# Expert rows weighted as they leave PSUM, routing weights scattered to the rows' places, and gathers that add into the residual

## The reference, cut to what matters

```python
logits = xt @ gate_w                       # xt = rmsnorm(h), 1024 tokens, 8 experts
topv, topi = jax.lax.top_k(logits, 2)
probs = jax.nn.softmax(topv, axis=-1)      # two weights for each token
for e in range(8):                         # F = 1024
    hh = jax.nn.silu(xt @ w1[e]) * (xt @ w3[e])
    out = out + w[:, e:e+1] * (hh @ w2[e])  # w holds the token's weight for e, or 0
x = layernorm(x + h + out)
```

## Time and profile before

| | us |
|---|---|
| median of 3 runs | 1451.32 |
| the runs | 1441.35, 1451.32, 1457.49 |
| profiled execution | 1436.41 |
| its span | 1434.8 |

### The profile page before, as it was taken

How to read it: one execution, slowest core, us unless ns; L and a number is a source line. 1 busy time by engine, 2 the same in 40 slices (tenths; PEclk the granted TensorE clock), 3 DMA queues, 4 the chain that set the end, 5 groups by cost and what they waited for, 6 DMA issues and landing times. The chain is left out here.

```text
span 1434.8 us, 24588 instructions
## 1 busy us (share of the span) xinstructions
PE 1318.0 (92%) x7943; PEld 716.3 (50%) x7943; DVE 1023.8 (71%) x1966; ACT 809.0 (56%) x1460; POOL 367.8 (26%) x602
## 2 busy tenths in 40 slices
PE   7988999999999999998687999999866999999993
PEld 4444444444444444443344555555434566666771
DVE  5847777777777777778568787888677655666676
ACT  5547666666666666666427566665653453455552
POOL 5402020201010111103256465664334100000025
PEclk9999999999999999999699999999987999999997
DMA  8317676657675767588264353535474765777653
GB/s 251 60 37 146 134 126 121 146 111 148 117 153 105 151 115 150 108 184 145 98 206 71 71 143 61 132 70 97 87 201 149 247 216 198 235 237 235 221 144 122
DMA packets 451869, 206.18 MB, mean 144 GB/s; under 512 B 401089, under 2 KB 415425, under 8 KB 451777
## 3 DMA queue, kind: packets, MB, share of 16 engines
q1 hardware_dynamic: 448640, 196.67, 57.7%
q0 software_dynamic: 2560, 8.39, 1.8%
q10 hardware_dynamic: 576, 0.00, 0.0%
HBM read 87.38 MB, written 16.45 MB: 72 GB/s over the span
## 5 line engine op out<-in xcount | busy, mean ns | idle before, releaser
L1453 DVE SCALAR_TENSOR_TENSOR X<-xa_SC,xa_rs,X 128x1024 f16<-128x1024 f32 x128 | 164.4, 1284 | 98.3 <-issue 97.6
L1276 ACT ACTIVATE X<-xa_SC,xa_rs 128x1024 f16<-128x1024 f32 x128 | 147.1, 1149 | 110.5 <-POOL xa_rs L1007 110.5
L1145 PE MATMUL xa_psS<-xa_KT,xa_QT 128*128 128x512 f16 x768 | 186.4, 379 | 6.1 <-DVE xa_mn L1485 4.7
L1157 PE MATMUL xa_psO<-wide,xa_V 128*128 128x512 f16 x768 | 173.6, 383 | 7.0 <-DMA wide<-X 6.9
L1007 POOL TENSOR_SCALAR xa_rs<-xa_rc,flag 128x1 f32<-128x1 f32 x128 | 33.9, 265 | 517.0 <-DVE xa_rc L1446 517.0
L1485 DVE CUSTOM_DVE_ANT_0 xa_SC<-xa_psS,maskb 128x1024 f32<-128x1024 f32 x128 | 155.1, 1212 | 4.5 <-PE xa_psS L1145 2.4
L1298 ACT ACTIVATE xa_SC<-xa_SC,xa_mn 128x1024 f32<-128x1024 f32 x128 | 145.5, 1136 | 13.4 <-DVE xa_mn L1485 13.3
L1157 PEld LDWEIGHTS xa_psO<-wide,xa_V 128*128 128x128 f16 x768 | 74.6, 98 | 102.2 <-issue 17.1
L1145 PEld LDWEIGHTS xa_psS<-xa_KT,xa_QT 128*128 128x128 f16 x768 | 73.4, 98 | 90.7 <-DVE xa_mn L1485 9.4
L1298 ACT ACTIVATE sa_SC<-sa_SC,sa_mn 128x128 f32<-128x128 f32 (+3 forms) x128 | 71.5, 558 | 78.1 <-DVE sa_mn L1485 78.0
L1944 PE MATMUL rmoe_psG<-rmoe_XGT,W 128*128 128x352 f16 (+6 forms) x768 | 109.0, 292 | 2.1 <-DVE rmoe_XGT L2052 2.1
(11 more groups left out here) (291 smaller groups left out, 2271.7 us busy)
## 6 DMA issues: line engine op xcount, KB each, us to landing
first<-in_L_ffn_w_dram SPq DMA_DIRECT2D x12, 2048.0 KB, 11.6
W2raw<-in_L_ffn_w_dram SPq DMA_DIRECT2D x8, 2048.0 KB, 9.1
expert_rows_dram<-zeros SPq DMA_DIRECT2D x10, 512.0 KB, 9.4
xa_WPraw<-in_L_xattn_Wq_dram SPq DMA_DIRECT2D x8, 512.0 KB, 11.1
xa_WOraw<-in_L_xattn_Wo_dram SPq DMA_DIRECT2D x8, 512.0 KB, 4.5
first<-in_L_ffn_wq_dram SPq DMA_DIRECT2D x4, 1024.0 KB, 7.6
first<-in_L_ffn_wo_dram SPq DMA_DIRECT2D x4, 1024.0 KB, 5.8
first<-in_L_ffn_w_dram SPq DMA_DIRECT2D x8, 512.0 KB, 6.8
```

Of the source, the lines that this page charges most:

```text
L1145: last = nc.tensor.matmul(psS[j % NSC][:, c:c + cw], QT[b][:, hq, g, t * P:(t + 1) * P], KT[b][:, hk, c:c + cw], start=(q == 0), stop=(q = ...
L1157: last = nc.tensor.matmul(psO[:, c:], V[b][:, hv, blk, :], PT[g % NPT][:, blk, hp, c:], start=(blk + q == 0), stop=(blk == NBLK - 1 and q ...
L1276: nc.scalar.activation(PN[j % NPN][:, 0:w // P, 0, :], by_block(SC[j % NSC], w), ACT.Identity, scale=rs[:, j % 4:j % 4 + 1]).then_inc(norm ...
L1453: nc.vector.scalar_tensor_tensor(out=PN[j % NPN][:, 0:w // P, 1, :], in0=by_block(SC[j % NSC], w), scalar=rs[:, j % 4:j % 4 + 1], in1=PN[j ...
```

## The change

The routing weight is multiplied into an expert's rows when they are copied out of PSUM, instead of when they are added to the residual.

- For this the weights have to stand in the order of the expert's rows. The first WT_ROWS = 5 rows of XG (2560 numbers) become a list of weights, and all rows of experts move up by 5. POOL issues 16 more scatters of one number for each of 128 tokens, ahead of the 16 scatters of rows.
- SP reads the list back into `row_wt`, one DMA for each of the 20 row tiles of experts 0 to 6 (`TILES_BEFORE[LAST]`), one number for each partition. They stand after the first loads of w1 and w3 and ahead of its wait for `scattered`.
- VectorE's copy of psY becomes a multiplication by `row_wt`; where `packs`, one more multiplication follows the addition. Before the first of them it waits for the 20 loads.
- The 16 gathers add into X directly (`compute_op=ALU.add`). All eight of choice 0 come first, then all of choice 1, each waiting for the earlier gather of its tile; in the first eight each waits for the one four tiles back.
- `combine` and its 16 instructions are gone; `finish_rows(t)` waits for the two gathers of tile t.
- One more clearing DMA of 5 rows of YG stands in the attention stage before.

```diff
-FIRST_ROW = tuple(sum(CAPS[:p]) for p in range(E))
+WT_ROWS = -(-sum(CAPS) // (D - 1))
+FIRST_ROW = tuple(WT_ROWS + sum(CAPS[:p]) for p in range(E))
...
+        row_wt = sb("row_wt", [P, LAST, CTL], F32)
+        WG = XG.rearrange("n d -> (n d)")[0:WT_ROWS * D].rearrange("(n o) -> n o", o=1)
...
+            def load_weights(p):
+
+                for r in range(TILES[p]):
+                    at, w = FIRST_ROW[p] + r * P, width(p, r)
+                    sp.dma_start(row_wt[0:w, p, r:r + 1], WG[at:at + w, :]).then_inc(wt_in, 16)
...
                     if first:
+                        sp.wait_ge(wt_scattered, 16 * 2 * NT)
+                        for q in range(LAST):
+                            load_weights(q)
                         sp.wait_ge(scattered, 16 * 2 * NT)
                         sp.wait_ge(pad_zeroed, 1)
                     load_rows(p + 1)
...
             pool.wait_ge(slots_done, 1)
             for t in range(NT):
                 for k in range(2):
+                    pool.indirect_dma_start(out=WG, out_offset=bass.IndirectOffsetOnAxis(ap=slots[:, k, t:t + 1], axis=0),
+                                            in_=p12[:, k, t:t + 1], in_offset=None).then_inc(wt_scattered, 16)
+            for t in range(NT):
+                for k in range(2):
                     pool.indirect_dma_start(out=XG, out_offset=bass.IndirectOffsetOnAxis(ap=slots[:, k, t:t + 1], axis=0),
                                             in_=XPF[:, t, :], in_offset=None).then_inc(scattered, 16)
...
-            for t in range(NT):
-                if t >= 2:
-                    pool.wait_ge(gathered[t - 2], 32)
-                for k, dst in enumerate((Y1, Y2)):
-                    pool.indirect_dma_start(out=dst[:, t, :], out_offset=None, in_=YG[0:ROWS, :],
...
+            for k in range(2):
+                for t in range(NT):
+                    if k:
+                        pool.wait_ge(gathered[t], 16)
+                    elif t >= 4:
+                        pool.wait_ge(gathered[t - 4], 16)
+                    pool.indirect_dma_start(out=X[:, t, :], out_offset=None, in_=YG[0:ROWS, :],
+                                            in_offset=bass.IndirectOffsetOnAxis(ap=slots[:, k, t:t + 1], axis=0),
+                                            compute_op=ALU.add).then_inc(gathered[t], 16)
...
-            def combine(t, ks=(0, 1)):
-
-                for k in (ks,) if isinstance(ks, int) else ks:
-                    dve.wait_ge(gathered[t], 32)
-                    wait_from(dve, combined, 2 * t + k)
-                    nc.vector.scalar_tensor_tensor(out=X[:, t, :], in0=(Y1, Y2)[k][:, t, :], scalar=p12[:, k, t:t + 1],
-                                                   in1=X[:, t, :], op0=ALU.mult, op1=ALU.add).then_inc(combined, 1)
...
                     if first and r == 0:
                         dve.wait_ge(x_added, NT)
+                        dve.wait_ge(wt_in, 16 * TILES_BEFORE[LAST])
...
-                        nc.vector.tensor_tensor(YR[0:w, r, :], psY[r % 2][0:w, :], folded[0:w, :],
-                                                ALU.add).then_inc(y_copied, 1)
+                        nc.vector.tensor_tensor(folded[0:w, :], psY[r % 2][0:w, :], folded[0:w, :],
+                                                ALU.add).then_inc(summed, 1)
+                        dve.wait_ge(summed, i + 1)
+                        nc.vector.tensor_scalar(YR[0:w, r, :], folded[0:w, :], wt, None, ALU.mult).then_inc(y_copied, 1)
                     else:
-                        nc.vector.tensor_copy(YR[0:w, r, :], psY[r % 2][0:w, :]).then_inc(y_copied, 1)
+                        nc.vector.tensor_scalar(YR[0:w, r, :], psY[r % 2][0:w, :], wt, None, ALU.mult).then_inc(y_copied, 1)
...
+        cleared.append((YG[0:WT_ROWS, :], zeros[0:WT_ROWS, :], zeroed))
```

More of the change, by code:

```diff
@@ L34 @@
 CAPS = (352, 352, 336, 304, 288, 272, 256, 240)
-FIRST_ROW = tuple(sum(CAPS[:p]) for p in range(E))
+WT_ROWS = -(-sum(CAPS) // (D - 1))
+FIRST_ROW = tuple(WT_ROWS + sum(CAPS[:p]) for p in range(E))
 TILES = tuple(-(-c // P) for c in CAPS)
 TILES_BEFORE = tuple(sum(TILES[:p]) for p in range(E + 1))
-ROWS = sum(CAPS)
+ROWS = WT_ROWS + sum(CAPS)
 PINNED = 16384.0
@@ L1910, in _ @@
             pool.wait_ge(scattered, 16 * 2 * NT)
-            for t in range(NT):
-                if t >= 2:
-                    pool.wait_ge(gathered[t - 2], 32)
-                for k, dst in enumerate((Y1, Y2)):
-                    pool.indirect_dma_start(out=dst[:, t, :], out_offset=None, in_=YG[0:ROWS, :],
-                                            in_offset=bass.IndirectOffsetOnAxis(ap=slots[:, k, t:t + 1], axis=0)
-                                            ).then_inc(gathered[t], 16)
+            for k in range(2):
[7 more added lines that the diff above has]
+                                            compute_op=ALU.add).then_inc(gathered[t], 16)
             for i in range(NT):
@@ L2096, in step @@
                                                 ALU.is_equal).then_inc(chosen_done, 1)
-                if last:
-                    for t in range(3):
-                        combine(t)
                 for r in range(TILES[p]):
@@ L2104, in step @@
                                                 YH[0:width(p, r), r, 0, :], ALU.subtract).then_inc(y_lo, 1)
-                        if r == 0:
-                            for t in range(3, 6):
-                                combine(t)
-                        else:
+                        if r:
                             finish_rows(r - 1)
@@ L2121, in step @@
                         dve.wait_ge(folded_done, i + 1)
-                        nc.vector.tensor_tensor(YR[0:w, r, :], psY[r % 2][0:w, :], folded[0:w, :],
-                                                ALU.add).then_inc(y_copied, 1)
+                        nc.vector.tensor_tensor(folded[0:w, :], psY[r % 2][0:w, :], folded[0:w, :],
+                                                ALU.add).then_inc(summed, 1)
+                        dve.wait_ge(summed, i + 1)
+                        nc.vector.tensor_scalar(YR[0:w, r, :], folded[0:w, :], wt, None, ALU.mult).then_inc(y_copied, 1)
                     else:
-                        nc.vector.tensor_copy(YR[0:w, r, :], psY[r % 2][0:w, :]).then_inc(y_copied, 1)
+                        nc.vector.tensor_scalar(YR[0:w, r, :], psY[r % 2][0:w, :], wt, None, ALU.mult).then_inc(y_copied, 1)
             def finish_rows(t):
                 dve.wait_ge(part_ready, t + 1)
-                dve.wait_ge(combined, 2 * t + 2)
+                dve.wait_ge(gathered[t], 32)
                 nc.vector.scalar_tensor_tensor(out=X[:, t, :], in0=part_bank[t][:, :], scalar=last_wt[:, t:t + 1],
@@ L2182, in _ @@
             for t in range(TILES[LAST] - 1, NT):
-                if t + 5 < NT:
-                    combine(t + 5)
                 finish_rows(t)
```

7 lines of the change are left out of this document (4 added, 3 removed).

## The result

| | before | changed |
|---|---|---|
| median, us | 1451.09 (20 runs, 1441.35 to 1457.49) | 1454.71 (20 runs, 1450.64 to 1463.16) |
| profiled execution, us | 1436.41 | 1457.36 |
| its span, us | 1434.8 | 1455.8 |

The changed kernel takes 1.0042 [1.0028, 1.0057] of the time before: 3.6 us more by the medians, within 1%. The forecast was 1455, 4 us more. The two profiled executions stand 21 us apart, though, and the rest of this document is about that gap. The forecast met the median, but what the traces show before expert 1 and in the tail is not what it priced.

What follows compares the result with a forecast made beforehand. TensorE was taken to bound nearly all, VectorE the tail after the last up stage. Tail -4.4, stall +6.8 and clock +1.7 sum to +4.1 us: 1451.3 + 4 = 1455 us, range 1446 to 1468.

Steps and rivals of the forecast that it cites:

- So the tail gives -4.4 us, if the gathers are in time: After the last up stage: without the 16 combines the eighth `finish_rows` starts at 1418.8 instead of 1423.23.
- from below it costs what a plain one costs: POOL in the tail: lower assumption for a gather that adds, taken at 1.25 us for each issue.
- gathers that add are the bound: Rival, chance 0.14: in the tail `finish_rows` waits for slow gather transfers; with the stall +14 to +26 us, 1465 to 1478.
- POOL's queue of scatters: POOL before expert 1: weights from 1092.48, row scatters moved past 16 issues, from 1117.0 to a last start at 1137.8.
- Now 20 weight loads come first: SP's queue before expert 1's row loads: 20 weight loads take 7.8 us, to 1136.4, hidden behind the scatters.
- Weights of four bytes are dear: Rival, chance 0.08: a weight load costs SP 1.0 us, +11 us, 1462; at 2.0, +31.
- The stall before expert 1: TensorE waits for `turned` before expert 1: 6.8 us, from a shift of 10.4 less 3.6 of room.
- 1.7 for the clock: TensorE's first matmuls of expert 1 after the wait run at the 1.2 GHz level: +1.7 us.
- The lower bound of 0.5 us for the stall: Low end of the 0.5 to 17.5 us range given for TensorE's stall before expert 1.
- Costs put at nothing: VectorE's multiplications, the W2raw load of expert 1 issued 3.5 us later against TensorE, and the clearing DMA: no cost.
- Checks it set itself: Wrong if idle before expert 1 is under 2 or over 12 us, or the tail's chain names the gathers.
- Three of its other signs: SP's row loads first issued at 1141 to 1142; tail 4.4 us shorter; no VectorE wait for an indirect DMA.

Runs made afterwards that it cites:

- e_no_weights: Changed kernel without the weight scatters and loads, `row_wt` filled with a constant (routing weights left out): 1437.63 us, 1.0013 of the kernel before.
- e_nw_early: As e_no_weights, with the adding gathers no longer waiting for the middle of the last up stage: 1434.40 us, 0.9901 of the kernel before.
- e_pitch: Changed kernel with its 4-byte weights written 512 bytes apart in a DRAM tensor of their own: 1448.60 us, 1.0091 of the kernel before.
- e_spread: Changed kernel with weight scatters of 512 bytes for each token into a DRAM tensor of their own: 1461.80 us, 1.0094 of the kernel before.
- after_again: The changed kernel, unedited, profiled a second time on another chip: 1453.09 us (one run), 1.012 of the kernel before.
- e_small_after: Changed kernel with weight scatters behind the row scatters, no weight loads, `row_wt` constant (routing weights left out): 1458.66 us, 1.0063 of the kernel before.
- e_shift: Kernel before with 24 memsets on POOL ahead of its row scatters, no small writes added: 1459.59 us, 1.0066 of the kernel before.
- e_plain_gather: Changed kernel with the two-buffer plain gathers and combines of before, factor 1.0 for the weight: 1453.10 us, 1.0115 of the kernel before.
- e_early_gather: Changed kernel, whole, with adding gathers no longer waiting for the middle of the last up stage: 1449.19 us, 1.0085 of the kernel before.

## Why the prediction was right, and where it was not

**The total** was right on the chip of the record: 4 us forecast, 3.6 measured. The sum behind it was -4.4 + 6.8 + 1.7. The traces read +0.8 in the tail and +19.7 before expert 1, 20.5 together, and a ratio of 1.012 on another chip. The forecast added its 4 us to a median of 1451 that stood 15 us above the profiled execution, which no run of that set reached; of the changed kernel the profiled execution (1457.4) is already above the median (1454.7). So the number was met with a sum that was 16 us short of what the traces show, and a baseline that was 15 us above the trace that the sum was read from. That the two nearly cancelled is luck: no run shows why the medians on that chip stand only 3.6 us apart.

**"So the tail gives -4.4 us, if the gathers are in time": the condition failed.** The step at fault is "from below it costs what a plain one costs", applied to POOL: 1.25 us for each issue, where 1.84 was measured. At 1.25 the 16 end at about 1407, at the first row scale; at 1.84 the changed kernel's end 20.5 us after the start of the down stage, and the scales of all tiles queue behind them. The forecast looked for a late gather where `finish_rows` waits for it, in VectorE, and there the waits are 1.2 us in all: the eighth `finish_rows` starts 24.9 us after the down stage does, 2.0 more than forecast. It didn't ask what else stands behind the gathers on POOL, which costs the other 3.2: the last normalisation ends 7.0 us after that start and not 3.8 as before. Together they are the 5.2 us between the 26.8 that the forecast's -4.4 gives and the 31.96 measured. The rival "gathers that add are the bound" had the right place in the kernel but the wrong resource: it priced the transfer. The rule it quoted (the Trainium skill, Collectives: The Full Stack, The bandwidth ceiling: the fold count and why AG ≠ RS ≠ AR), given there for reductions between cores, says that an add needs two source reads and so runs at half a copy's rate. The estimate from e_no_weights, 1.7 us against 0.81, agrees with it, and the transfer was not the bound, as forecast. e_nw_early shows 4.2 of the 4.4 us once POOL starts earlier.

**POOL's queue of scatters: right.** Weights from 1091.9, rows from 1116.1 to a last start of 1135.5 (forecast 1092.5, and 1117.0 to 1137.8).

**SP's queue: wrong in its first line.** The step "Now 20 weight loads come first", done by 1136.4, took for granted that SP is free at 1128.6, when its loads of w1 and w3 are done. They take 29 to 34 us in the three kernels with the packed list ahead of the rows, 28 with it behind them, and 16 to 20 in all others. The loads of the weights themselves were sized well: 9.7 us for 20 against 7.8.

**"Weights of four bytes are dear"** had the right suspect and the wrong victim: a weight load costs SP 0.48 us with its gap, under the 0.65 from which it would have counted; what is dear is the write, and the one that pays is every other transfer at that time. The rule given there (the Trainium skill, DMA: Bandwidth & Descriptors, Specifications: under 512 bytes the engine reads, modifies and writes) doesn't tell the cases apart. e_pitch writes the same four bytes and its w1/w3 loads take 17.3 us, e_spread writes 512 and they take 16.5.

**The stall before expert 1**, forecast 6.8 with 1.7 for the clock: the mechanism is there in e_pitch, where SP's w1/w3 loads are not slowed. Row loads at 1143.48 (forecast 1141.6), transposes 4.6 us later (5.0), `turned` some 6 us on, and TensorE waits 4.2 us for it and 2.9 before that at psY, 7.1 in all. The wait at psY was not forecast: VectorE's first multiplication waits 2.5 us for the weights, since their loads take 12.3 us in this kernel. TensorE in e_pitch:

```profile
1142.95 7.07 PE L1984 MATMUL rmoe_psY<-W,rmoe_HT 128*96 128x512 f16 x24 [2.86 <-DVE X L2137]
1154.17 3.46 PE L1966 MATMUL rmoe_psG<-rmoe_XGT,W 128*128 128x352 f16 x12 [4.15 <-DMA rmoe_XGT<-X]
```

The clock in e_pitch, from the windows:

```profile
1154.00:1156.00 2.00, 1.83 (x8) 1.02 (x9) 0.00 (x0) 0.00 (x0) 0.00 (x0) 0.61 0.82 252
1156.00:1158.00 2.00, 2.00 (x9) 1.07 (x8) 0.00 (x0) 0.00 (x0) 0.00 (x0) 0.53 0.98 338
1158.00:1160.00 2.00, 2.00 (x15) 1.31 (x14) 0.00 (x0) 0.37 (x1) 0.00 (x0) 1.00 0.94 256
```

After the wait the granted clock is near half for about 4 us, the 1.2 GHz level, and `mid` grows by 1.7 us, the forecast's figure. The lower bound of 0.5 us for the stall doesn't follow from its own terms: 1137.5, 2.3 and 6.0 give 1145.8, where TensorE started before, so no stall. The clock took its toll a second time, which was not forecast: after the wait at psY the 24 matmuls take 7.07 us instead of 5.2 (a third of 15.70, as before expert 1 in the trace of the kernel before).

In the changed kernel itself this mechanism stands in the shadow of the late w1/w3: in after_again the wait for `turned` is 0.8 us. The clock's part is there too, behind the other wait: 2.3 us on the last 24 matmuls of expert 0.

**Costs put at nothing**: `mid` is 250.08 with and without the multiplications, so they cost nothing, and neither does the later W2raw load: in e_pitch it is issued 1.9 us ahead of expert 1, as forecast, and what `mid` grew by is the clock's.

**Checks it set itself.** It called itself wrong if the idle time before expert 1 was over 12 us, or if the chain in the tail named the gathers. Both happened, with the median as forecast: TensorE stands for 14.7 us in expert 0's up stage in the profile and for 14.0 before expert 1 in after_again, and POOL's gathers hold 2% of the chain. Three of its other signs failed: SP's first row load came at 1147.33 and not at 1141 to 1142, the tail was not shorter, and VectorE did wait for indirect DMAs.

## What to carry to other kernels

Look, when a DMA is given more to do, at how long its issue holds the engine that writes its descriptors and at what stands behind it in that engine's queue; the transfer may be hidden and the issue not. Two thousand 4-byte writes into one packed list slowed the other transfers of the moment here; writing them 512 bytes apart in a buffer of their own did not, and sparing the list was better still. When the median stands 15 us off the profiled execution, a forecast from that profile that meets the median has not been confirmed by it: compare trace with trace, stage by stage, and from the same chip.

## What the runs showed of the hardware that was not expected

- Packed small writes: 2048 writes of 4 bytes into 10 KB stretched 4096-byte packets of another queue from 0.24 us to 1.2 to 4.9 us on average and SP's four w1/w3 loads of 1 MB from 16.5 to 19.8 us together to 28.4 to 34.0. Which part of the memory path is held was not shown, nor whether it is the packing or the shared buffer.
- An indirect gather of 128 rows of 2 KB holds POOL for 1.54 us when it adds and 0.95 when it doesn't; a scatter holds it for about as long whether it carries 2 KB or 4 bytes a row (medians of 0.96 and 0.99 in the changed kernel).
- Stops without a shown cause. In traces from the chips on which the kernel before takes 1449 to 1451 us, TensorE, VectorE and ScalarE stop or crawl together for 12 to 22 us at a time in the routed stage (changed kernel 1115 to 1137, e_small_after in the same place, e_spread at 1130 to 1142, e_shift at 1128 to 1141 and 1403 to 1421), with TensorE at times issuing one or a few matmuls every 1.4 us. None of the eight traces from the chips at 1436 has one. Of e_nw_early, on a slower chip, the trace has none, and its median (1434.4) is 15 us below that of before there; the first trace of the kernel before has none either, but its chip isn't on record. ScalarE's idle time in these stops is put down to DMAs of earlier stages or to "remote" (16.9 us in the changed kernel), which says nothing sure. All four traces with a stop are of kernels with a longer POOL queue ahead of expert 1, so that may be what brings a stop on; but after_again, e_plain_gather, e_early_gather and e_pitch have it too, on other chips, and no stop. It fits that most executions of the kernel before on those chips have such a stop, and that in the changed kernel it falls into time that is lost to the slow loads anyway: that would make the change 17 us dearer on one chip and 4 on the other. No run shows it; what the engines wait for in a stop, and where the 15 us of the kernel before lie, stays open.
